# Twenty one-hot comparisons of each index search, moved from VectorE to GpSimd

## The chip, the cores and the metric
The kernel runs on one core of one Trainium2 chip. The metric is the device time of one execution in microseconds (us); lower is better. The kernel before took 3496.7 us (median of three runs, 3490.24 to 3497.87).

A core has five engines with a queue of instructions each: PE (TensorE, matrix products), DVE (VectorE), ACT (ScalarE), POOL (GpSimd) and SP (SyncE, which only starts transfers here). Each works its own queue in order; between engines only semaphores order the work.

## The reference
```python
scores = jnp.einsum('bhqd,bhkd->bhqk', q, k) * scale       # b=2, h=16, 4096 x 4096
sparsity = scores.max(axis=-1) - scores.mean(axis=-1)
_, top_idx = jax.lax.top_k(sparsity, U)                    # U = 307 queries of 4096
q_sel = jnp.take_along_axis(q, top_idx[..., None], axis=2)
scores_sel = jnp.einsum('bhud,bhkd->bhuk', q_sel, k) * scale
attn = jax.nn.softmax(scores_sel, axis=-1)
out_sel = jnp.einsum('bhuk,bhkd->bhud', attn, v)
out = jnp.zeros_like(q).at[bi, hi, top_idx].set(out_sel)
...
x = _layernorm(x + attention)
x = _layernorm(x + feed_forward(x))                        # token shift, sigmoid gate, squared relu
```
For each of the 32 pairs of batch and head the full score matrix is needed only for its row maxima. The 307 best queries are then found, attended for and written back.

## The kernel before
**Rounds.** The score matrices are worked through in 2048 rounds ("main" in the plan), 64 for a head. One round is a tile of 128 queries by 2048 key columns, folded into half of that: PE makes two products into CP (line 592) and two into DP (line 596), ACT takes the absolute value of CP into AB (line 858, two of 128x512), and DVE forms the sum of DP and AB and its maximum along the row in one instruction (line 1014, called the reduction here, 128x1024). AB has three buffers and DP two, so the engines can be only a few rounds apart. One reduction in each round makes the start of line 1014 a clock for the whole kernel.

**Beside the rounds** the function `schedule` writes out one plan, a list of tokens; every engine walks through it and emits what it has to do for each token. Between two rounds stand at most a few tokens from three generators: `selection` (the search for the 307 queries), `attention`, and `background` (projections, values, and the feed-forward part of batch 0). The heads are split into seven groups of 8, 5, 3, 5, 5, 3 and 3. A group's search starts when its last row maximum is there. Groups 0 to 5 are searched beside the rounds; group 6 is searched behind the last of them, in the tail.

**The search** (`select`) finds the cut value digit by digit (ACT compares, PE counts), marks the chosen queries, and ranks them by prefix sums on PE. The rank minus one is the slot of a query, 0 to 306. `slots` splits it: slot & 15 into fb, slot >> 4 into fa, both 128 partitions by 32 x n columns, where n is the group's number of heads: 256, 160, 96, 160, 160 and 96 columns for groups 0 to 5. Then come the one-hot tables: `ob` writes 16 comparisons of fb with 0 to 15 into OB on DVE (line 1144), which POOL multiplies by the token number (line 1360); `oa` writes 20 comparisons of fa with 0 to 19 into OA (line 1149). Beside the rounds both come two to a round: eight rounds of `ob`, then ten of `oa`. Four rounds later `idx` multiplies OA by OB on PE (line 667, 32 small products for a head), which puts each token number in its slot; the first of them waits for all of `sel_tk` and `sel_oa`. DVE adds an offset (line 1155), and `ixdma` stores the indices. SCR is the memory in which OA, OB and the attention buffers EL lie.

**Attention** for a head takes one step of 128 keys in a round: PE makes scores (line 688), ACT takes exponentials (line 896), POOL subtracts the upper half of each number to keep the rest as a second f16/bf16 operand (line 1411, EL), and six steps later PE multiplies both with the values (lines 703, 704). There are ten buffers. At the end of a head DVE normalizes (1170 to 1176), POOL adds a bias (1420) and starts three indirect DMAs (1424). `qgzero`, once, clears two areas of SCR on POOL (1368, 1369) behind group 0's search.

**Feed-forward beside the rounds** (`feed`, batch 0): a tile of 128 tokens advances by one stage in some nine rounds. POOL has most of its elementwise work: token shift (1475, 1477, 1480), squared relu (1490), normalization (1430 to 1435, 1462, 1511), sums (1445, 1498). PE's projection (726, W_rT) waits for the token shift (`f_mx`), and POOL's 1490 waits for ACT's relu (942). These stages run beside the searches of groups 3 and 4; attention runs beside those of groups 1, 2 and 5.

POOL's queue is ordered by the plan too. Within a round the tokens of `selection` stand ahead of those of `attention` or `background`. In group 3 the token shift of tile 13 stands ahead of the first comparison, and that of tile 14 behind the 18th. In group 4 the token shift of tile 28 stands ahead of all, and that of tile 29 behind the 14th.

Of the kernel before, what the change touches and what calls it, by code (L numbers as in the profile page):

```python
# [9 lines left out]
ALU = mybir.AluOpType  # L10
ACT = mybir.ActivationFunctionType

NB, L, D, H, DH = 2, 4096, 256, 16, 16
NT = L // 128
# [7 lines left out]
GROUPS = [(0, 0, 8), (0, 8, 5), (0, 13, 3), (1, 0, 5), (1, 5, 5), (1, 10, 3), (1, 13, 3)]  # L22
# [32 lines left out]
def schedule():  # L55
# [9 lines left out]
    def bank():  # L65
        while True:
            state["turn"] += 1
            b = spare[state["turn"] % len(spare)]
            if b != state["open"]:
                return b  # L70
# [49 lines left out]
    def select(g):  # L120
        n = GROUPS[g][2]
        gaps = 0 if tail[0] else 1
        on = "D" if tail[0] else "A"
        yield [("flip", g, bank())]
        for _ in range(gaps):
            yield []
        yield [("parts", g)]
        for _ in range(2 * gaps):
            yield []
        for i, (_, w) in enumerate(DIGITS):  # L130
            if gaps:
                for j in range(w):
                    yield [("cmp", g, i, j, on)] + ([("sel", g, i)] if j == 0 and i < n else [])
            else:
                yield [("cmp", g, i, j, on) for j in range(w)] + ([("sel", g, i)] if i < n else [])
            bk = bank()
            yield [("cnt", g, i, bk), ("digit", g, i, on, bk)]
            for _ in range(gaps):
                yield []
        for _ in range(2 * gaps):  # L140
            yield []
        yield [("cut", g, bank())]
        for _ in range(3 * gaps):
            yield []
        yield [("need", g, bank())]
        yield [("rank1", g, bank())]
        for _ in range(4 * gaps):
            yield []
        yield [("rank2", g, bank())]
        yield [("slots", g)]  # L150
        for _ in range(3 * gaps):
            yield []
        m = 2 if gaps else 4
        for j in range(0, 16, m):
            yield [("ob", g, j, m)]
        for j in range(0, A_COLS, m):
            yield [("oa", g, j, m)]
        for _ in range(4 * gaps):
            yield []
        for h in range(n):  # L160
            yield [("idx", g, h, bank())]
        yield [("ixdma", g)]
# [96 lines left out]
    def selection():  # L259
        for g in range(len(GROUPS)):  # L260
            while ("c", g) not in done or "p1" not in done:
                yield None
            state["search"] = True
            yield from select(g)
            state["search"] = False
            yield from prelude(g)
# [7 lines left out]
    for n in range(NB * H):  # L274
# [21 lines left out]
        if n + 1 in HEAD0:  # L296
            g = HEAD0.index(n + 1) - 1
# [20 lines left out]
def attention_rwkv(nc, x, Wq, bq, Wk, bk, Wv, bv, Wo, bo, W_r, W_k, W_v, mu_r, mu_k, out):  # L318
    ctx = ExitStack()
    with ctx:  # L320
        def sb(name, shape, dt=F32):
            return ctx.enter_context(nc.sbuf_tensor(name, shape, dt))

        def sem(name):
            return ctx.enter_context(nc.semaphore(name))
# [43 lines left out]
        OA = SCR[:, 2048:4608].bitcast(F16).rearrange("p (a n) -> p a n", a=A_COLS)  # L369
# [3 lines left out]
        fa = sb("fa", [128, NT * 8], F16)  # L373
        fb = sb("fb", [128, NT * 8], F16)
        SPr = sb("SPr", [128, NT, 8, 2])
        SB = [sb(f"S{g}", [128, 2, n, 16]) for g, (_, _, n) in enumerate(GROUPS)]
        SS = [v[:].rearrange("p u h t -> p u t h") for v in SB]
        slotf = sb("slotf", [128, NT, 8])
# [35 lines left out]
        def ff_tiles(count, w=D):  # L414
# [40 lines left out]
        sel_sl, sel_f, sel_ob, sel_tk, sel_oa, sel_ix = (sem(n) for n in (  # L455
            "sel_sl", "sel_f", "sel_ob", "sel_tk", "sel_oa", "sel_ix"))
        arr, ah_pe, ah_act, s_pe, ex_act, el_g, el_d = (sem(n) for n in (
            "arr", "ah_pe", "ah_act", "s_pe", "ex_act", "el_g", "el_d"))
# [496 lines left out]
        def _(dve):  # L955
# [138 lines left out]
            def cut(g, bank):  # L1094
                n, _, (m1, m2, *_) = views(g)
                cf = BANK[bank][:, 0:16 * n].rearrange("p (h q) -> p h q", q=16)[:, :, 0]
                cf = cf.unsqueeze(1).unsqueeze(1).broadcast_to([128, 2, 16, n])
                m1, m2 = (m.rearrange("p (u t) h -> p u t h", u=2) for m in (m1, m2))
                dve.wait_ge(sel_pe, SEL0[g] + 18)
                after(dve, sel_m, 5 * g)  # L1100
                dve.tensor_tensor(m1, SS[g], cf, ALU.is_gt).then_inc(sel_m, 1)
                dve.tensor_tensor(m2, SS[g], cf, ALU.is_equal).then_inc(sel_m, 1)
# [6 lines left out]
            def rank1(g, bank):  # L1109
                n, _, (m1, m2, m3, *_) = views(g)  # L1110
                dve.wait_ge(sel_m, 5 * g + 3)
                dve.wait_ge(sel_pe, SEL0[g] + 20)
                q = seq.mark(dve.tensor_tensor(m3, BANK[bank][:, 0:NT * n].rearrange("p (t h) -> p t h", h=n),
                                               need[:, 0:n].unsqueeze(1).broadcast_to([128, NT, n]), ALU.is_le))
                dve.wait_ge(q_dve, q)
                q = seq.mark(dve.tensor_tensor(m3, m3, m2, ALU.mult))
                dve.wait_ge(q_dve, q)
                dve.tensor_tensor(m3, m3, m1, ALU.add).then_inc(sel_m, 1)
# [24 lines left out]
                for j in range(j0, j0 + m):  # L1143
                    dve.tensor_scalar(OB[:, j, 0:NT * n], fb[:, 0:NT * n], float(j), None, ALU.is_equal).then_inc(sel_ob, 1)

            def oa(g, j0, m):
                n = GROUPS[g][2]
                for j in range(j0, j0 + m):
                    dve.tensor_scalar(OA[:, j, 0:NT * n], fa[:, 0:NT * n], float(j), None, ALU.is_equal).then_inc(sel_oa, 1)

# [95 lines left out]
            def f9(b, t, late):  # L1246
                if late:
# [5 lines left out]

            stages = dict(xt=xt, kbar=kbar, kmm=kmm, split=split, val=val, main=main, cap=capture, parts=parts, cmp=cmp,
                          digit=digit, cut=cut, need=need_, rank1=rank1, rank2=rank2, slots=slots, ob=ob, oa=oa, idx=idx,
                          st=st, otr=otr, f2=f2, f3=f3, f5=f5, f7=f7, f8=f8, f9=f9)
            for stage, *args in plan:
# [4 lines left out]
        def _(pool):  # L1262
# [91 lines left out]
            def ob(g, j0, m):  # L1354
                n = GROUPS[g][2]
                tk = tokc[:].unsqueeze(2).broadcast_to([128, NT, n])
                for j in range(j0, j0 + m):
                    v = OB[:, j, 0:NT * n].rearrange("p (t h) -> p t h", h=n)
                    pool.wait_ge(sel_ob, 16 * g + j + 1)
                    pool.tensor_tensor(v, v, tk, ALU.mult).then_inc(sel_tk, 1)  # L1360

            def qgzero():
                pool.wait_ge(l_s[0], 32 * 24)
                pool.wait_ge(l_s[1], 32 * 24)
                pool.wait_ge(l_q, 16 * 16)
                pool.wait_ge(xt_pe, 32)
                pool.wait_ge(s_lo, 48)
                pool.memset(QG, 0.0)
                pool.wait_ge(q_pool, seq.mark(pool.memset(QST, 0.0)))
# [136 lines left out]
            def f9(b, t, late):  # L1506
                if not late:
# [2 lines left out]
                    pool.wait_ge(f_r2, k + 1)  # L1510
                    pool.tensor_scalar(fo[k % 4], fo[k % 4], r[:, 0:1], r[:, 1:2], ALU.mult, ALU.add).then_inc(f_o3, 1)

            stages = dict(vones=vones, qzero=qzero, split=split, slots=slots, ob=ob, qgzero=qgzero, gath=gath, arr=arrange,
                          st=st, put=put, f1=f1, f2=f2, f3=f3, f5=f5, f6k=f6k, f7=f7, f8=f8, f9=f9)
            setup()
            for stage, *args in plan:
# [153 lines left out]
```

## Time and profile before
| | us |
|---|---|
| median of three runs (range) | 3496.7 (3490.24 to 3497.87) |
| profiled execution | 3497.08 |
| its span, first to last instruction | 3495.3 |
| PE busy | 3113.3 (89%) |
| DVE busy | 2940.5 (84%) |
| ACT busy | 2878.4 (82%) |
| POOL busy | 1491.0 (43%) |
| mean granted clock of PE, share of full speed | 0.968 |

Busy time counts the time in which an engine runs an instruction. A share over the whole span hides that each stretch has its own bound, and a wait inside an instruction, such as one for a shared port, counts as busy. Times in a timeline are counted from the start of the span.

### The profile page before, as it was taken

Reading aid. Unit: us, or ns where it says so; the run is one execution under the profiler, and the core shown is the slowest. Engines: PE = TensorE matmul, PEld = TensorE weight load, DVE = VectorE, ACT = ScalarE, POOL = GpSimd, SP = SyncE. Lnnn points to the kernel's source line nnn. Section 1 sums busy time; section 2 is a strip of 40 time slices with the busy share of each in tenths; the row PEclk is TensorE's granted clock in tenths of the full one; section 3 lists DMA queues with packets and bytes.
Section 4 is the critical chain, followed back from the end, with each engine's and each line's share of the span. In section 5 each row is a group of like instructions: output and inputs, shape, how many; then the busy total and the mean of one; then the engine's idle time right before and its main releaser. Section 6 shows DMA issues by size and latency. Waiting matters only on the chain.

```text
span 3495.3 us, 58965 instructions
## 1 busy us (share of the span) xinstructions
PE 3113.3 (89%) x15985; PEld 1442.4 (41%) x15985; DVE 2940.5 (84%) x5954; ACT 2878.4 (82%) x6445; POOL 1491.0 (43%) x2634
## 2 busy tenths in 40 slices
PE   5999999998899998998999888899988898897588
PEld 3334333343244433433444444544444443344366
DVE  2889988899978888888898888888887888886478
ACT  3889888889779999899899877699976699894455
POOL 2210022100136643453556455675555653457754
PEclk8999999999989999999999999999999999997899
DMA  6432232316122241241111241121141222013022
GB/s 183 147 81 36 61 85 76 82 36 15 25 38 38 38 33 27 37 33 31 23 38 29 43 48 42 42 44 36 31 38 42 40 32 31 14 20 15 14 77 69
DMA packets 262295, 163.64 MB, mean 47 GB/s; under 512 B 167563, under 2 KB 241483, under 8 KB 257867
## 3 DMA queue, kind: packets, MB, share of 16 engines
q1 hardware_dynamic: 255819, 158.50, 24.8%
q0 software_dynamic: 6144, 1.37, 0.5%
q8 instruction: 128, 2.10, 0.3%
q14 instruction: 204, 1.67, 0.2%
HBM read 111.86 MB, written 47.86 MB: 46 GB/s over the span
## 4 chain that ended last, share of the span: by engine, by line
PE 32%; ACT 26%; issue 19%; DVE 19%; POOL 2%; DMA 1%; SPq 0%; DVEq 0%; ACTq 0%; POOLq 0%
ACT AB L858 19%; DVE JK L1014 11%; PE CP L592 10%; PE DP L596 9%; ACT E L896 4%; ACT msk L879 2%; PE PV L703 2%; PE PV L704 2%; PE BP L688 2%; DVE SPr L1014 1%; PE PV L540 1%; DVE fst L1184 1%; PE BP L726 1%; PE BP L540 1%; DVE VF L1222 1%
## 5 line engine op out<-in xcount | busy, mean ns | idle before, releaser
L1014 DVE CUSTOM_DVE_ANT_0 JK<-DP,AB 128x1024 bf16<-128x1024 f32 x2048 | 2469.0, 1222 | 384.7 <-DVE SPr L1014 137.7
L858 ACT ACTIVATE AB<-CP 128x512 f32<-128x512 f32 x4096 | 2227.3, 598 | 306.8 <-PE CP L592 253.6
L592 PE MATMUL CP<-KS,QS 128*128 128x512 f16 x4096 | 1425.3, 389 | 96.3 <-ACT AB L858 20.5
L596 PE MATMUL DP<-KS,QS 128*128 128x512 f16 x4096 | 1241.9, 385 | 70.4 <-DVE SPr L1014 63.7
L1411 POOL TENSOR_TENSOR SCR<-E 128x307 f16<-128x307 f32 x968 | 672.5, 706 | 590.7 <-ACT E L896 581.8
L592 PEld LDWEIGHTS CP<-KS,QS 128*128 128x128 f16 x4096 | 393.8, 97 | 883.7 <-ACT AB L858 762.3
L596 PEld LDWEIGHTS DP<-KS,QS 128*128 128x128 f16 x4096 | 361.6, 98 | 402.9 <-DVE SPr L1014 187.3
L896 ACT ACTIVATE E<-BP 128x307 f32<-128x307 f32 x883 | 384.5, 436 | 55.1 <-PE BP L688 53.7
L1266 POOL TENSOR_SCALAR SCR<-SCR 128x48 f16<-128x48 f16 (+2 forms) x122 | 49.6, 406 | 571.7 <-DVE SCR L982 321.6
L688 PE MATMUL BP<-QT,KA 128*128 128x307 f16 x883 | 263.1, 298 | 20.9 <-ACT QT L888 19.1
L703 PE MATMUL PV<-E,XT 128*128 128x307 bf16 x512 | 161.4, 316 | 34.2 <-POOL SCR L1411 34.0
L1014 DVE DVE_READ_ACCUMULATOR2_ANT SPr<- 128x1 f32 x2048 | 168.9, 82 | 0.0
L704 PE MATMUL PV<-SCR,XT 128*128 128x307 f16 x512 | 157.6, 308 | 0.0
L703 PE MATMUL PV<-E,VF 128*128 128x307 bf16 x512 | 153.9, 301 | 0.0
L704 PE MATMUL PV<-SCR,VF 128*128 128x307 f16 x512 | 149.7, 292 | 0.0
L688 PEld LDWEIGHTS BP<-QT,KA 128*128 128x128 f16 x883 | 87.0, 98 | 147.3 <-issue 24.2
L1384 POOL DMA_INDIRECT SCR<-QN,idxs x96 | 99.6, 1037 | 77.2 <-issue 70.4
L1424 POOL DMA_INDIRECT AO<-OG,idxs x96 | 100.8, 1050 | 34.1 <-issue 16.9
L896 ACT ACTIVATE E<-DP 128x307 f32<-128x307 f32 x115 | 47.4, 427 | 48.3 <-PE DP L688 48.1
L1430 POOL TENSOR_SCALAR frs<-fmv 128x1 f32<-128x1 f32 x128 | 29.1, 227 | 132.3 <-DVE fmv L1186 129.6
L703 PEld LDWEIGHTS PV<-E,XT 128*128 128x128 f16 x512 | 52.1, 102 | 80.4 <-POOL SCR L1411 32.7
L1431 POOL TENSOR_TENSOR frs<-frs,halfc 128x1 f32<-128x1 f32 x128 | 78.3, 612 | 10.7
(381 smaller groups left out, 2984.5 us busy)
## 6 DMA issues: line engine op xcount, KB each, us to landing
KS<-KTC SPq DMA_DIRECT2D x256, 128.0 KB, 5.0
QS<-QSC SPq DMA_DIRECT2D x512, 64.0 KB
KA<-KTC SPq DMA_DIRECT2D x128, 128.0 KB, 3.8
QN<-SCR SPq DMA_DIRECT2D x16, 544.0 KB, 3.4
SCR<-in_L_attn_x SPq DMA_DIRECT2D x16, 512.0 KB, 6.8
KTC<-SCR SPq DMA_DIRECT2D x32, 256.0 KB, 2.2
QSC<-SCR SPq DMA_DIRECT2D x32, 256.0 KB, 2.3
AO<-E SPq DMA_DIRECT2D x2, 4096.0 KB, 21.9
```

The source lines that it names most:

```text
L592: pe.matmul(o, qs, ks[j][:, 1, :], start=True, stop=True).then_inc(sc_c, 1)
L596: r = pe.matmul(o[:, 512 * j:512 * j + 512], qs, ks[j][:, 0, :], start=True, stop=True)
L688: pe.matmul(o[:, 0:U], KA[hx % 2][:, 128 * kc:128 * kc + 128], QT[hx % 2][:, 0:U], start=True, stop=True).then_inc(s_pe, 1)
L703: pe.matmul(PV[:, 0:U], v, EH[a % NE], start=kc == 0, stop=False)
L704: pe.matmul(PV[:, 0:U], v, EL[a % NE], start=False, stop=kc == NT - 1).then_inc(pv_pe, 1)
L858: act.activation(AB[p % 3][:, 512 * j:512 * j + 512], BANK["C%d" % j], ACT.Abs).then_inc(ab_full, 1)
L896: act.activation(E[a % NE][:], BANK[bank][:, 0:U], ACT.Exp, scale=2 * SCALE / (WS * WS)).then_inc(ex_act, 1)
L1014: dve.tensor_tensor_reduce(out=JK[p % 2][:], in0=BANK["D%d" % u], in1=AB[p % 3][:], scale=1.0, scalar=-3.0e38, op0=ALU.add, op1=ALU.max, a ...
L1384: pool.indirect_dma_start(out=QG[0:w, 3 * (hx % 8) + c, :], out_offset=None, in_=QNr[b], in_offset=bass.IndirectOffsetOnAxis(ap=ixf[0:w, k ...
L1411: pool.tensor_tensor(EL[a % NE], E[a % NE][:], EH[a % NE], ALU.subtract).then_inc(el_g, 1)
L1424: pool.indirect_dma_start(out=AOr[b], out_offset=bass.IndirectOffsetOnAxis(ap=ixf[0:w, k:k + 1], axis=0), in_=OG[i][0:w, c, :], in_offset= ...
L1431: i = pool.tensor_tensor(r[:, 0:1], r[:, 0:1], halfc[:], ALU.pow)
```

## The change
The 20 comparisons of `oa` go from DVE to POOL in groups 0 to 5. The plan stays as it is but for a flag in the token: "A" beside the rounds, "D" in the tail. DVE skips the token where the flag is "A"; POOL skips it where it is "D". On POOL each `oa` token first waits for fa and fb, which POOL itself writes. The 16 comparisons of `ob` stay on DVE.

```diff
         for j in range(0, A_COLS, m):
-            yield [("oa", g, j, m)]
+            yield [("oa", g, j, m, on)]
...
-            def oa(g, j0, m):
+            def oa(g, j0, m, on):
                 n = GROUPS[g][2]
+                if on == "A":
+                    return
                 for j in range(j0, j0 + m):
                     dve.tensor_scalar(OA[:, j, 0:NT * n], fa[:, 0:NT * n], float(j), None, ALU.is_equal).then_inc(sel_oa, 1)
...
+            def oa(g, j0, m, on):
+                n = GROUPS[g][2]
+                if on == "D":
+                    return
+                pool.wait_ge(sel_f, g + 1)
+                for j in range(j0, j0 + m):
+                    pool.tensor_scalar(OA[:, j, 0:NT * n], fa[:, 0:NT * n], float(j), None, ALU.is_equal).then_inc(sel_oa, 1)
```
POOL's table of stages gets the new function as well.

## Rows read from the trace of the kernel before

**Rows 1.** The page, its first part: busy us (share of the span) xinstructions.
```profile
PE 3113.3 (89%) x15985; PEld 1442.4 (41%) x15985; DVE 2940.5 (84%) x5954; ACT 2878.4 (82%) x6445; POOL 1491.0 (43%) x2634
```

**Rows 2.** Windows of groups 0 to 5: length, busy PE PEld DVE ACT POOL, clock, DMA.
```profile
939.40:956.50 17.10, 11.97 (x41) 3.48 (x40) 17.08 (x42) 10.85 (x21) 4.17 (x4) 0.90 0.00 1
1418.60:1436.40 17.80, 13.87 (x65) 5.17 (x63) 17.73 (x46) 14.39 (x30) 10.33 (x15) 1.00 0.02 3
1710.60:1725.30 14.70, 14.06 (x68) 6.07 (x69) 14.59 (x44) 13.83 (x31) 7.59 (x11) 1.00 0.01 2
2221.20:2238.50 17.30, 14.34 (x67) 7.24 (x66) 17.20 (x48) 12.00 (x26) 14.29 (x35) 1.00 0.07 23
2730.40:2748.90 18.50, 15.47 (x63) 7.62 (x62) 17.25 (x47) 11.57 (x25) 15.66 (x37) 0.91 0.04 15
3034.50:3051.60 17.10, 14.53 (x63) 6.55 (x64) 15.17 (x42) 11.54 (x25) 9.73 (x21) 0.80 0.00 1
```

**Rows 3.** The same view: four plain rounds of group 0; ten rounds with attention.
```profile
956.50:961.07 4.57, 3.99 (x25) 1.38 (x24) 4.57 (x8) 3.72 (x7) 0.00 (x0) 1.00 0.00 0
1746.37:1759.85 13.48, 13.44 (x72) 6.23 (x72) 12.32 (x21) 13.40 (x31) 11.32 (x27) 1.00 0.54 80
```

**Rows 4.** Timeline of group 0: start, us, engine, line, operation (idle before in brackets).
```profile
940.55 3.19 DVE L1149 TENSOR_SCALAR SCR<-fa 128x256 f16<-128x256 f16 x2
...
940.94 2.66 POOL L1369 MEMSET SCR<- 128x3072 f16 x1
...
953.67 1.22 DVE L1014 CUSTOM_DVE_ANT_0 JK<-DP,AB 128x1024 bf16<-128x1024 f32 x1
...
955.08 1.22 DVE L1014 CUSTOM_DVE_ANT_0 JK<-DP,AB 128x1024 bf16<-128x1024 f32 x1
```

**Rows 5.** Timeline of group 1: DVE beside POOL.
```profile
1419.53 2.67 POOL L1411 TENSOR_TENSOR SCR<-E 128x307 f16<-128x307 f32 x4
...
1420.86 1.21 DVE L1014 CUSTOM_DVE_ANT_0 JK<-DP,AB 128x1024 bf16<-128x1024 f32 x1
...
1431.96 1.08 POOL L1424 DMA_INDIRECT AO<-OG,idxs  x1 [0.30 <-issue]
...
1432.31 2.82 DVE L1149 TENSOR_SCALAR SCR<-fa 128x160 f16<-128x160 f16 x2
```

**Rows 6.** Timeline of group 5: its first pair of comparisons.
```profile
3035.69 1.62 DVE L1149 TENSOR_SCALAR SCR<-fa 128x96 f16<-128x96 f16 x2
```

**Rows 7.** Groups by form on POOL: count | busy us, mean ns | idle before.
```profile
L1431 POOL TENSOR_TENSOR frs<-frs,halfc 128x1 f32<-128x1 f32 x128 | 78.3, 612 | 10.7
L1360 POOL TENSOR_TENSOR SCR<-SCR,tokc 128x160 f16<-128x160 f16 x48 | 20.9, 459 | 3.8 <-DVE SCR L1144 2.4
L1332 POOL TENSOR_SCALAR SCR<-SCR 128x512 f16<-128x512 f16 x12 | 7.4, 618 | 0.0
L1266 POOL TENSOR_SCALAR fa<-sloti 128x160 f16<-128x160 int32 x3 | 1.0, 325 | 14.8 <-DVE sloti L1133 14.8
```

**Rows 8.** Timeline of group 1: a subtraction, its first use, the first index matmul.
```profile
1412.85 0.70 POOL L1411 TENSOR_TENSOR SCR<-E 128x307 f16<-128x307 f32 x1
...
1418.84 0.30 PE L703 MATMUL PV<-E,VF 128*128 128x307 bf16 x1
...
1442.45 1.54 PE L667 MATMUL BP<-SCR 128*20 128x16 f16 x32
```

**Rows 9.** Timeline of groups 3 and 4: POOL's token shift and the matmul behind it.
```profile
2234.06 0.61 POOL L1490 TENSOR_TENSOR VF<-VF 128x256 f32<-128x256 f32 x1 [1.95 <-ACT VF L942]
...
2238.48 0.73 POOL L1480 TENSOR_TENSOR VF<-VF 128x256 f32<-128x256 f32 x1
...
2242.20 0.41 PEld L726 LDWEIGHTS BP<-W_rT,VF 128*128 128x128 f32 x2
...
2740.47 0.61 POOL L1490 TENSOR_TENSOR VF<-VF 128x256 f32<-128x256 f32 x1 [1.48 <-ACT VF L942]
...
2745.73 0.67 PE L726 MATMUL BP<-W_rT,VF 128*128 128x256 f32 x2 [0.43 <-POOL VF L1480]
```

## What the change does to the time, predicted

> **What bounds the kernel now.** I read the page first: in 3495.3 us TensorE (PE) is busy 89%, VectorE (DVE) 84%, ScalarE (ACT) 82% and GpSimd (POOL) 43% [rows 1]. An average like this names no bound, so the stretches in which the 120 moved comparisons stand come next. There is one for each of the groups 0 to 5, ten rounds long, with two comparisons in each round; the view of windows gives the busy time of each engine in them [rows 2]. DVE is busy 17.08 of 17.10 us in group 0, 17.73 of 17.80 in group 1, 14.59 of 14.70 in group 2, 17.20 of 17.30 in group 3. There it is DVE that ends last. In groups 4 and 5 it has gaps (17.25 of 18.50, 15.17 of 17.10). POOL is the other column to read: 4.17, 10.33 and 7.59 us in groups 0 to 2, 9.73 in group 5, but 14.29 and 15.66 us in groups 3 and 4, because the feed-forward part of batch 0 runs on it at that time.
>
> Then I asked what a round costs once the comparisons are gone. Right behind the comparisons of group 0, four rounds take 4.57 us, 1.14 each: the reduction alone, back to back [rows 3]. With attention beside it ten rounds take 13.48 us, and ACT is busy 13.40 of them, so 1.35 a round is ACT's pace [rows 3]. Those are the two floors.
>
> **What the change removes.** Undisturbed, a round with two comparisons of 256 columns takes 1.41 us from one reduction to the next (953.67 to 955.08), and one without takes 1.14 [rows 3, 4]. The disturbed ones are worth more. In group 0 one pair is 3.19 us long, while POOL clears two areas, the larger in 2.66 us [rows 4]. In group 1 one pair takes 2.82 us while POOL works through four subtractions without a gap [rows 5]. In group 5 the first pair takes 1.62 us [rows 6].
> A page of the Trainium skill (SBUF — State Buffer, "SBUF: two separate sides") says that a DVE operation which uses both ports and a POOL instruction exclude each other for one whole instruction. The trace agrees that they exclude each other, but the pair in group 1 waits for about three of POOL's instructions, not one. By the page it would have cost about 1.3 us less, and the gain there would be smaller by as much. The measured pair is the one I use.
> POOL's comparisons should not hold up the reductions that stay on DVE: the one at 1420.86 starts while POOL is inside four subtractions in a row and takes its usual 1.21 us [rows 5].
>
> Group by group, from the length of the stretch now to the length after:
> - Group 0, no attention beside it: 17.1 us become ten rounds of 1.14, 11.4. **Minus 5.6.** POOL does its 20 comparisons first (8 us at the price below, to about 949) and clears afterwards, when DVE has no comparison left to block. The index matmuls come four rounds behind the stretch, 939.4 + 11.4 + 4.6 = 955.4, well behind POOL's last comparison.
> - Group 1: 17.8 become 13.5 at ACT's pace [rows 2, 3]. **Minus 4.3.**
> - Group 2: 14.7 become 13.5. **Minus 1.2.**
> - Group 5: the pair of 1.62 us goes, less 0.1 that it overlaps with its neighbours and the 0.2 by which ACT's floor lies above DVE's (1.35 against 1.14): **minus 1.3**. A plain pair of 96 columns fits between the two floors, so the other nine rounds gain nothing; much of this stretch is at a low clock (0.80 on the mean [rows 2]) and PE's.
>
> **What it adds.** POOL has no comparison with a constant in this trace, and no operation of one step on more than two columns. Its one-input operations of two steps cost 325 ns at 160 columns and 618 at 512 [rows 7], 0.83 ns a column. I take 0.34 us at 160, 0.28 at 96 and 0.40 at 256, the line through these two rows and a little for the other form. Below, I see 0.29. Above stands the two-input product of 160 columns at 459 ns [rows 7]; and the power function, at 612 ns for a single column [rows 7], shows that the kind of operation can matter on POOL, so a tail reaches to 0.7. All in all POOL gets 60 x 0.34 + 40 x 0.28 + 20 x 0.40, near 40 us. What matters is where POOL is late.
> The Trainium skill (GPSIMD Engine Reference, Elementwise) gives about 1.8 cycles for an element at best, and 769 ns for 512 elements. This case's 128x512 row says 618 [rows 7], faster. By the page 160 columns would be near 0.42 us (an estimate) and the sum below near minus 5.2 us.
>
> - Groups 1, 2, 5: a step of attention asks POOL for one subtraction (four in 2.67 us, 0.67 each [rows 5]); with two comparisons that is 1.35 in a round of 1.35. POOL neither falls behind nor catches up. The subtraction that ended at 1413.55 is first used by the matmul at 1418.84 [rows 8], so 5 us of delay cost nothing. The index matmuls of group 1, which now wait for POOL's comparisons, start at 1442.45 [rows 8]. POOL works from 1419.5 through 20 comparisons (6.8), some nine subtractions (5.9) and an addition with three indirect DMAs of 1.08 and gaps of 0.3 (4.5 [rows 5]) and is done near 1436.7, while PE comes there near 1438.2 (1442.45 - 4.3). **Nothing added**, but with 1.5 us to spare only.
> - Group 3: PE waits for POOL at the projection of each feed-forward tile (line 726 behind line 1480). Two such hand-overs lie around the stretch. The earlier one has none of the new comparisons in front of it in POOL's queue. In front of the later one stand 18. Now it ends on POOL at 2239.21 (2238.48 + 0.73) and is used at 2242.20, 3.0 us of slack, and POOL waited 1.95 us for ACT on the way there [rows 9]. 18 x 0.34 = 6.1, less 1.95 of idle time, puts the end at 2243.4: PE is 1.3 us later than before, though DVE was relieved of 20 comparisons. **Plus 1.3.**
> - Group 4: the same hand-over has no slack at all. PE waits already now for POOL (0.43 us, released at 2745.7), and POOL idled 1.48 us on the way [rows 9]. 14 comparisons precede it: 14 x 0.34 = 4.8, less 1.48. **Plus 3.3.** The index matmuls of groups 3 and 4 stand behind these hand-overs in PE's queue and come later by the same amount, which leaves POOL the time for its last two to six comparisons.
> The later hand-overs come behind the index matmuls, which hold up PE and let POOL catch up, so the delay isn't paid twice. The tail (group 6) keeps its comparisons on DVE.
>
> **Sum.** -5.6 - 4.3 - 1.2 - 1.3 + 1.3 + 3.3 = -7.8 us. The profiled execution took 3497.1 us (a span of 3495.3 and 1.8 around it), against a median of 3496.7 for the three timed runs: 3497.1 - 7.8 = **3489.3 us**. A difference under 0.2%, 7 us, can hardly be told from no change here, and the forecast lies just beyond that.
>
> **Rivals.**
> 1. *POOL is never late.* If the feed-forward hand-overs absorb the delay, because POOL's work in front of them shrinks or PE is held up elsewhere, groups 3 and 4 gain too: 17.3 and 18.5 us become about 14.6 and 15.5, which is PE's busy time there (14.34 and 15.47 [rows 2]). That gives -12.4 - 2.7 - 3.0 = -18.1, 3479.0 us. Against it speak the 0.43 us wait and POOL's 15.66 us of work in 18.50. Chance 0.13.
> 2. *The comparison is dearer, slower than before.* Groups 3 and 4 pay 18 + 14 = 32 comparisons of 160 columns: each 0.1 us more costs 3.2 us. From 0.42 the margin in group 1 is gone too: PE then waits in front of the index matmuls for POOL's last comparison, and 20 x (price - 0.42) of the gain there goes, up to all 4.3. At 0.459 the sum is -7.8 + 3.8 + 0.8 = -3.2 us (3493.9); at 0.52 it is zero, and from there on the kernel is slower. At 0.7 it is -7.8 + 11.5 + 4.3 = +8.0, 3505 us. One mechanism: POOL's queue sets when PE goes on. For it speaks that no such operation is in the trace and the row of 612 ns; against it, that all wide one-input rows lie on one line. Chance of a price of 0.42 to 0.52: 0.18; above it 0.11, of which 0.08 lie over 0.67, where the loss reaches 7 us.
> 3. *The change does nothing.* If every round were held by ACT or PE at the same time and DVE's busy time only looks full, the time stays 3497. The 3.19 and 2.82 us pairs, in which PE stood still, speak against it. Chance 0.06.
> The forecast has 0.52, and carries its own spread of some 4 us: the granted clock falls to half in many short stretches (0.90 to 0.91 on the mean in groups 0 and 4, 0.80 in group 5 [rows 2]), and new waits of PE in groups 3 and 4 may add such a fall, the one avoided in group 0 take one away.
>
> **Range and chances.** From rival 1 to just short of the dearest comparison: 3478 to 3500 us. Faster by over 0.2% (under 3489.7): 0.13 of rival 1 and 0.38 of the forecast's 0.52 (more than half, for its spread reaches further down, to falls of the clock that are avoided), 0.51. Slower by over 0.2% (above 3503.7): 0.08. The same: 0.41, from the rest of the forecast, the price of 0.42 to 0.67 and rival 3.
>
> **What would show each step.** In the profile after, rounds of 1.14 us in group 0's stretch and no DVE instruction over 2 us there; ten rounds near 13.5 us in groups 1 and 2; POOL's comparisons of 160 columns at 0.34 us; waits of PE line 726 for POOL line 1480 grown from 0.43 us to 3 or more in group 4 and new in group 3, and ten rounds of groups 3 and 4 longer than before. The prediction is wrong if POOL's comparison costs 0.45 us or more, if PE's index matmuls wait for it, or if the feed-forward hand-overs show no wait.

## The result, and the profile after

The changed kernel takes 3520.4 us (median of four runs, 3519.8 to 3523.5) against 3495.9 for the kernel before beside it: a ratio of 1.0074, 95% interval 1.0057 to 1.0092. It is slower by 24.5 us in the medians, 26 by the ratio, where 7.8 us less were forecast. The profiled execution has a span of 3518.0 us against 3495.3.

The page after, busy time of the engines, answers to [rows 1]:

```profile
PE 3120.8 (89%) x15985; PEld 1444.1 (41%) x15985; DVE 2920.8 (83%) x5834; ACT 2876.4 (82%) x6445; POOL 1561.6 (44%) x2754
```

120 instructions went from DVE to POOL. DVE is busy 20 us less and POOL 71 us more, where the prediction had added 40. The groups by form on POOL (count | busy us, mean ns | idle before) say why. Line 1370 is the moved comparison, 1362 the product that was line 1360:

```profile
L1370 POOL TENSOR_SCALAR SCR<-fa 128x160 f16<-128x160 f16 x60 | 36.5, 612 | 3.9
L1362 POOL TENSOR_TENSOR SCR<-SCR,tokc 128x160 f16<-128x160 f16 x48 | 20.9, 459 | 3.8 <-DVE SCR L1144 2.4
L1370 POOL TENSOR_SCALAR SCR<-fa 128x96 f16<-128x96 f16 x40 | 18.0, 452 | 2.6
L1370 POOL TENSOR_SCALAR SCR<-fa 128x256 f16<-128x256 f16 x20 | 16.9, 847 | 1.3
```

A comparison of 160 columns costs 612 ns, not 340; from 96 to 256 columns it grows by 2.5 ns a column, where the line through [rows 7] grows by 0.83. That line also left out rows of the kernel before (count | busy us, mean ns | idle before):

```profile
L1475 POOL TENSOR_SCALAR VF<-VF,cols 128x128 f32<-128x128 f32 x128 | 47.8, 374 | 0.0
L1462 POOL TENSOR_SCALAR VF<-VF,frs 128x256 f32<-128x256 f32 x32 | 17.6, 552 | 0.1
```

Both are multiply-adds too, but with a factor read from a column of memory instead of a constant. By the line they would cost 298 and 404 ns. So it was not true that all wide one-input rows lie on one line, which rival 2 had as its reason against a dearer comparison.

Next the windows of the same ten rounds in groups 0 to 5, which answer to [rows 2] (length; busy PE, PEld, DVE, ACT, POOL with counts; clock, DMA share, GB/s):

```profile
938.80:950.20 11.40, 10.18 (x40) 2.93 (x38) 11.40 (x20) 10.27 (x20) 10.77 (x14) 1.00 0.00 0
1418.20:1431.50 13.30, 12.89 (x63) 5.44 (x62) 12.55 (x26) 12.51 (x28) 12.09 (x21) 1.00 0.01 2
1714.90:1728.50 13.60, 13.30 (x65) 5.68 (x66) 12.74 (x25) 12.87 (x29) 11.88 (x24) 1.00 0.00 1
2227.20:2241.80 14.60, 13.70 (x65) 7.10 (x64) 13.73 (x28) 11.59 (x25) 13.39 (x30) 1.00 0.06 20
2743.60:2768.90 25.30, 15.54 (x60) 7.39 (x59) 13.94 (x28) 10.68 (x23) 23.12 (x48) 0.80 0.02 6
3056.80:3072.40 15.60, 14.30 (x63) 6.53 (x64) 12.29 (x22) 11.36 (x25) 13.98 (x33) 0.79 0.00 2
```

The relief of DVE came as forecast: 17.1 us became 11.4 in group 0 (11.4 forecast), 17.8 became 13.3 in group 1 (13.5), 14.7 became 13.6 in group 2 (13.5). Group 3 even became shorter here, 14.6 instead of 17.3. Only group 4 pays in its own stretch, 25.3 instead of 18.5. The other losses stand behind the stretches. To see them, take the start of the same reduction in both traces; the shift after minus before is -0.6 us when the ranks of group 0 are ready, and then:

| from the start of the group's slots to the next group's | forecast | changed kernel |
|---|---|---|
| group 0 | -5.6 | +0.2 |
| group 1 | -4.3 | +4.7 |
| group 2 | -1.2 | +1.7 |
| group 3 | +1.3 | +7.3 |
| group 4 | +3.3 | +9.0 |
| group 5 and the tail | -1.3 | +0.4 |
| sum | -7.8 | +23.3 |

One trace isn't exact to the microsecond here: in two later runs whose groups 0 to 2 are those of the kernel before, the same three lines read -1.0, +3.2, +2.4 and +2.3, +0.3, +0.9. The timed runs by groups, below, are the firmer evidence.

The waits of the changed kernel (engine, line, waited for: us in total, times, longest) name the places:

```profile
PE PV L703 <- POOL SCR L1421: 37.4, 7, 11.0
PE PV L726 <- POOL VF L1500: 14.0, 2, 7.1
PE BP L667 <- POOL SCR L1370: 6.8, 3, 3.8
PE BP L726 <- POOL VF L1490: 3.3, 5, 1.1
```

and those of the kernel before:

```profile
PE PV L703 <- POOL SCR L1411: 34.0, 6, 10.9
PE BP L726 <- POOL VF L1480: 2.4, 3, 1.2
PE BP L726 <- POOL VF L1490: 1.7, 1, 1.7
```

New are 14 us in which PE waits for line 1500, the squared relu (1490 before), once in group 3 and once in group 4, 6.8 us in which the index matmuls wait for the comparisons, and 3.4 us for attention's subtractions. The token shift (1490, was 1480), on which the prediction set its two losses, grew by 0.9 us only.

The timeline of group 3 after (start, us, engine, line, operation, idle time before in brackets):

```profile
2243.35 5.40 POOL L1370 TENSOR_SCALAR SCR<-fa 128x160 f16<-128x160 f16 x8
...
2248.83 0.61 POOL L1500 TENSOR_TENSOR VF<-VF 128x256 f32<-128x256 f32 x1
...
2249.59 1.19 PE L726 MATMUL PV<-W_vT,VF 128*128 128x256 f32 x2 [6.94 <-POOL VF L1500]
...
2255.49 0.67 PE L726 MATMUL BP<-W_rT,VF 128*128 128x256 f32 x2 [0.70 <-POOL VF L1490]
...
2257.55 1.51 PE L667 MATMUL PV<-SCR 128*20 128x16 f16 x32 [0.54 <-POOL SCR L1370]
```

Eight comparisons in a row, 5.40 us, are 0.68 apart, more than their 0.61. Behind them stands the square for which PE has been waiting 6.9 us. By the time of the projection on which [rows 9] rest (2242.20 before, 2255.46 after) the rounds have lost what the forecast allowed for and 6 us more.

In groups 0 and 1 it is the index matmuls and a subtraction:

```profile
949.82 8.25 POOL L1370 TENSOR_SCALAR SCR<-fa 128x256 f16<-128x256 f16 x9
...
958.22 1.42 PE L667 MATMUL BP<-SCR 128*20 128x16 f16 x32 [3.83 <-POOL SCR L1370]
...
1438.54 0.42 PE L703 MATMUL PV<-E,VF 128*128 128x307 bf16 x1 [3.51 <-POOL SCR L1421]
...
1442.18 1.51 PE L667 MATMUL BP<-SCR 128*20 128x16 f16 x32 [1.27 <-POOL SCR L1370]
```

### The profile page after: what moved, and what is told of

Read it like the earlier page. It is cut to its first block, busy times and chain, and to the rows that moved or that the text cites. A ratio compares the mean times of both kernels' runs of the same rounds, so it can differ in the third digit from the quotient of the medians.

```text
span 3518.0 us, 58965 instructions
## 1 busy us (share of the span) xinstructions
PE 3120.8 (89%) x15985; PEld 1444.1 (41%) x15985; DVE 2920.8 (83%) x5834; ACT 2876.4 (82%) x6445; POOL 1561.6 (44%) x2754
## 4 chain that ended last, share of the span: by engine, by line
PE 25%; ACT 17%; issue 15%; DVE 11%; POOL 4%; DMA 1%; DVEq 0%; ACTq 0%; POOLq 0%; SPq 0%
ACT AB L858 11%; PE CP L592 8%; PE DP L596 7%; DVE JK L1014 5%; ACT E L896 3%; PE PV L703 2%; PE PV L704 2%; PE BP L688 2%; ACT msk L879 1%; POOL SCR L1370 1%; DVE fst L1186 1%; PE BP L726 1%; DVE VF L1224 1%; PE PV L726 1%; DMA SCR<-QN,idxs 1%
## 5 line engine op out<-in xcount | busy, mean ns | idle before, releaser
L688 PEld LDWEIGHTS BP<-QT,KA 128*128 128x128 f16 x883 | 86.9, 98 | 146.3 <-issue 25.5
```

Source lines behind the costliest of these rows:

```text
L688: pe.matmul(o[:, 0:U], KA[hx % 2][:, 128 * kc:128 * kc + 128], QT[hx % 2][:, 0:U], start=True, stop=True).then_inc(s_pe, 1)
```

## The experiments

Ratios are against the kernel before on the same chip, with their 95% interval; shifts are those of the reductions in the traces.

**What makes POOL's comparison dear.** Nothing of the network is left; ten one-input forms and a two-input product, six each at four widths (the loop is shortened here).

```diff
+for form in (one_cmp, one_mul, cmp_add, mul_add, sub_max, mul_cmp, cmp_mul, one_ge, one_max, cmp32, tt_mul):
+    for w in (96, 160, 256, 512):
+        for k in range(6): form(w)      # e.g. pool.tensor_scalar(out, in, 3.0, None, ALU.is_equal)
```

> Nothing of the network is computed here: x is copied to the output while POOL runs rows of one-input operations of ten forms and one two-input product, six of each at 96, 160, 256 and 512 columns. It asks what makes POOL's comparison dear (612 ns at 160 columns in the changed kernel, where 325 was the row for a multiply-add). Theory A, the one-step form is dear: a product with one constant costs what the comparison costs, near 0.61 us at 160, and a comparison followed by adding zero falls to 0.33. Theory B, comparing is dear: a one-step product costs 0.33 or less, and a comparison costs 0.6 with or without a second step. Theory C, both go through one slow routine and only multiply-add is quick: every form but multiply-add costs 0.6.

The groups by form at 160 columns (and two at 512). Line 47 is the comparison as the change writes it, 50 a product with one constant, 53 comparison then add, 56 multiply-add, 74 a maximum in one step, 77 the two-input product:

```profile
L47 POOL TENSOR_SCALAR BB<-A 128x512 f16<-128x512 f16 x6 | 8.7, 1486 | 0.1
...
L53 POOL TENSOR_SCALAR BB<-A 128x160 f16<-128x160 f16 x6 | 4.3, 747 | 0.1
...
L56 POOL TENSOR_SCALAR BB<-A 128x512 f16<-128x512 f16 x6 | 3.5, 617 | 0.1
L50 POOL TENSOR_SCALAR BB<-A 128x160 f16<-128x160 f16 x6 | 3.5, 607 | 0.1
...
L47 POOL TENSOR_SCALAR BB<-A 128x160 f16<-128x160 f16 x6 | 3.5, 606 | 0.1
...
L74 POOL TENSOR_SCALAR BB<-A 128x160 f16<-128x160 f16 x6 | 3.5, 604 | 0.1
...
L77 POOL TENSOR_TENSOR BB<-A,C 128x160 f16<-128x160 f16 x6 | 2.7, 485 | 0.1
...
L56 POOL TENSOR_SCALAR BB<-A 128x160 f16<-128x160 f16 x6 | 1.8, 325 | 0.1
```

Theory C holds. The price has nothing to do with comparing: a product with one constant costs the same 0.61 us. Multiply followed by add is the one quick form among the ten; every other form of one step costs 2.5 ns a column, and every other of two steps more, 747 ns at 160. All wide one-input rows of the kernel before were multiply-adds, and the line was drawn through those of them that have two constants: a special case. The run doesn't try multiply-adds with a column as factor.

**The comparison in two steps.**

```diff
-pool.tensor_scalar(OA[:, j, 0:NT * n], fa[:, 0:NT * n], float(j), None, ALU.is_equal)
+pool.tensor_scalar(OA[:, j, 0:NT * n], fa[:, 0:NT * n], float(j), 0.0, ALU.is_equal, ALU.add)
```

> The changed kernel with POOL's comparison written in two steps, is_equal and then add 0.0; the values are the same. Theory A (the one-step form is dear): 0.33 us at 160 columns, and by the sum of the prediction near -8 us against the kernel before, 3489. Theories B and C: the price stays near 0.61 us or rises, and the time stays near 3520, or a little above.

755 ns at 160 columns, and 3539.3 us: 1.0125 (1.0108 to 1.0142). 0.14 us more on each of 60 comparisons, 0.22 on 20 and 0.09 on 40 are 16.6 us of POOL, and the kernel loses another 16 to 19. So where POOL is late already, more of its time goes into the kernel's nearly in full.

**The price that was forecast.**

```diff
-pool.tensor_scalar(OA[:, j, 0:NT * n], fa[:, 0:NT * n], float(j), None, ALU.is_equal)
+pool.tensor_scalar(OA[:, j, 0:NT * n], fa[:, 0:NT * n], 0.0, 0.0, ALU.mult, ALU.add)
```

> The changed kernel with each of POOL's 120 comparisons replaced by a multiply-add with 0.0 of the same shape (the price that the prediction took, 0.33 us at 160 columns). The upper part of the slots then isn't computed, and in groups 0 to 5 the 307 first tokens are attended for instead of the chosen ones, with the same number of transfers. If the prediction failed in the price alone, this takes 3497 - 8 = 3489 us, with group 3 about 1 and group 4 about 3 us later than before. If taking work off DVE costs something by itself (an order of waits, falls of PE's clock), it stays above 3497.

0.9962 (0.9949 to 0.9976), 13.3 us less than before. POOL's operations cost 329, 276 and 413 ns. (In groups 0 to 5 the table is then all zeros, and the indices are the constants that the iota behind it gives.) This is the prediction with its price right: the forecast of 3489.3 was 5.6 us too high for it, 3483.7. From here to the changed kernel POOL's 120 operations cost 35.5 us more, and the kernel takes 37 to 39 more, again nearly one for one. Group by group the shifts are -4.3, -3.8, -0.1, -1.9, +3.8 and, in group 5 with the tail, -5.4. Group 4 loses as forecast (+3.3); group 3 gains where a loss of 1.3 was forecast, and group 5 gains 4 us more, but 3.3 of its gain come before its comparisons begin, so not from the change.

**DVE relieved, POOL nearly free.**

```diff
+if (g, j0) == (0, 0):
+    pool.wait_ge(q_pool, seq.mark(pool.memset(OA[:], 0.0)))
-pool.tensor_scalar(OA[:, j, 0:NT * n], fa[:, 0:NT * n], float(j), None, ALU.is_equal)
+pool.memset(OA[:, j, 0:1], 0.0)
```

> As the run with multiply-adds, but each of POOL's 120 operations is the clearing of a single column (about 0.1 us), and the table is cleared once, in group 0. This is what the relief of DVE is worth when POOL pays almost nothing. The prediction's first rival gives -18 us, 3479; if ACT or PE hold the rounds at the same time, less than 5 us are gained.

0.9956 (0.9939 to 0.9972), 3483.6, 14 to 15 us less than before: as much as with multiply-adds, so in the total POOL's part at 0.33 us was hidden. The interval reaches from 10 to 21 us and doesn't exclude the first rival's 18. The trace, with 11.1 us less, is below it: the ten rounds are 14.6 us long in group 3, as that rival had it, and 16.1 in group 4, where it had 15.5. In group 4 POOL's part does show: -1.1 us here against +3.8 with multiply-adds. These two runs also change the data (a table of zeros, the iota as in the run before); what that does by itself wasn't tested, but the mean granted clock is 0.968 in both, as before.

**Which groups lose.**

```diff
-yield [("oa", g, j, m, on)]
+yield [("oa", g, j, m, "D" if g in (3, 4) else on)]        # POOL in 0, 1, 2, 5
+yield [("oa", g, j, m, "D" if g in (0, 1, 2, 5) else on)]  # POOL in 3 and 4
```

> POOL makes the comparisons in groups 0, 1, 2 and 5, beside which only attention runs; in groups 3 and 4, beside the feed-forward stages, they stay on DVE. If the loss of each group is its own, this keeps 0.8 + 4.8 + 1.6 + 0.3 = +7.5 us of the changed kernel's 22.7 (shift of the rounds, from the two traces): 3504 us. If the loss sits in the feed-forward hand-overs alone, as the prediction had it, the time is 3490 or less.

> The complement: POOL makes the comparisons in groups 3 and 4 alone. If losses add up: +7.3 and +7.5 and some 1 us behind group 4, near +15 us, 3512. The price of 0.61 us in the prediction's own sum gives 18 x 0.61 - 1.95 - 3.0 = +6.0 for group 3 and 14 x 0.61 - 1.48 = +7.1 for group 4, +13 us together, 3510. If the loss were one of clock or of order that any shift of the plan brings, it would be far from both.

The first: 1.0026 (1.0016 to 1.0035), +9 us. The second: 1.0048 (1.0031 to 1.0065), +17 us; its trace loses 5.0 us in group 3 and 9.0 in group 4, against 7.3 and 9.0 in the changed kernel. The two add up to 1.0074, the whole change. So two thirds of the loss belong to groups 3 and 4, with the feed-forward hand-overs, and one third to groups that the prediction had as gains of 12.4 us.

**Clearing later.**

```diff
 def qgzero():
     ...
+    pool.wait_ge(sel_oa, A_COLS)
     pool.memset(QG, 0.0)
```

> The kernel before, with one wait more on POOL: it clears its two areas only when DVE's 20 comparisons of group 0 are through. Tests what the 3.19 us pair is worth: if it is a wait for POOL's clearing and on the path, the pair shrinks to 0.35 us and the time falls by 2.8 us, to 3494. If PE's stall there was covered by something later (the falls of the clock, the index matmuls), less than 1 us is gained.

0.9995 (0.9985 to 1.0004): no difference that this can tell, though the interval reaches to 5 us less and doesn't exclude the 2.8 expected. In the trace the long pair is 0.35 us like its neighbours and the stretch 2.9 us shorter, so the pair did wait for POOL's clearing. What follows it is larger than the effect: the eight rounds with the index matmuls of group 0, windows before, after and here:

```profile
961.07:984.03 22.96, 22.96 (x282) 13.78 (x281) 10.81 (x27) 8.70 (x16) 0.00 (x0) 0.67 0.32 59
```

```profile
954.79:984.17 29.38, 25.95 (x289) 14.62 (x290) 11.14 (x26) 8.68 (x16) 6.08 (x6) 0.54 0.24 45
```

```profile
958.50:976.70 18.20, 18.20 (x281) 12.89 (x278) 10.44 (x26) 7.91 (x15) 0.00 (x0) 1.00 0.16 45
```

The last column but two is the granted clock, 0.67, 0.54 and 1.00 of full speed (2.4 GHz; it falls to 1.2). The same eight rounds take 22.96 us, 29.38 with 3.83 of waiting in them, and 19.14 (to the end of the eighth; the window shown ends 0.9 us earlier). At full clock they would be 3.8 us shorter in the kernel before, and 6.4 in the changed one, after its wait is taken out. The run with POOL in groups 3 and 4 alone, whose group 0 is that of before, took 19.2 us as well; the one with half the comparisons of groups 3 and 4 on POOL, unchanged here too, took 24.7 at a clock of 0.56. So this stretch's time varies from run to run with the clock, by 5.5 us, without any change to it. All 14 traces of the network together: in the 11 in which no index matmul of group 0 waits for POOL, the eight rounds take 19.1 to 24.7 us at clocks of 1.00 to 0.56; in the three with such a wait (the changed kernel, the one in two steps, and POOL in groups 0, 1, 2 and 5) they take 25.5 us beside the wait, at 0.53 to 0.55. In the five index rounds of group 1 the 11 have 12.2 to 15.2 us at 1.00 to 0.60, the three 17.8 to 18.3 at 0.50.

**One comparison each, in groups 0, 1, 2 and 5.**

```diff
-for j in range(j0, j0 + m):      # DVE
+for j in range(j0, j0 + m, 2 if on == "A" else 1):
-for j in range(j0, j0 + m):      # POOL
+for j in range(j0 + 1, j0 + m, 2):
```

Groups 3 and 4 have the flag "D" (all on DVE), DVE's early return is gone, and POOL clears behind the comparisons as in the run before.

> In groups 0, 1, 2 and 5 each round gives one comparison to DVE and one to POOL, groups 3 and 4 stay on DVE, and POOL clears behind the comparisons. By rates alone both engines now fit in a round: POOL 0.67 + 0.59 = 1.26 us, DVE 1.14 + 0.15 = 1.29, ACT 1.35. Then group 0 gains 4.5 (rounds of 1.28, and no 3.19 us pair), group 1 some 4, groups 2 and 5 one to three each: -9 to -12 us, 3486. If DVE's remaining comparisons now wait for POOL's slow ones (they exclude each other, 0.6 us each), nothing is gained: 3495 or more.

0.9969 (0.9959 to 0.9979), 10.8 us less. The first expectation was right: the ten rounds are 14.1 us long in group 1 and 13.9 in group 2, a little over ACT's pace, so DVE's remaining comparisons do wait at times, but cheaply.

**The index matmuls later.**

```diff
-for _ in range(4 * gaps):
+for _ in range(12 * gaps):       # between oa and idx, in the changed kernel
     yield []
```

> The changed kernel with twelve empty rounds instead of four between a group's comparisons and its index matmuls. If PE's waits for POOL in front of the index matmuls (3.8 us in group 0, 1.3 in group 1) and the falls of its clock behind them are a cause, groups 0 and 1 give back some 6 and 4 us, and groups 3 and 4, whose loss sits at feed-forward hand-overs, stay at about +7 each: 3520 - 8 = 3512 us. If the index matmuls were slow for another reason, the rows behind them stay as long as in the changed kernel and the time at 3520. Starting attention eight rounds later in each group may cost some of it in the tail.

1.0009 (0.9999 to 1.0020), 3498.6: better than either theory said. No index matmul waits for a comparison any more, and by the start of group 3 the rounds are 19 us ahead of before where the changed kernel is 6 behind. 11 us of that are given back behind the last reduction; that attention, started later, is left over is the likely reason. Groups 3 and 4 lose 3.7 and 8.6 us, nearly as before in group 4. The kernel is 22 us faster than the changed one without those waits, so they and what follows them are the likely cause in groups 0 to 2; part of the 19 us is only work put off, and this run doesn't separate them.

**One comparison a round on POOL in groups 0, 1, 2 and 5.**

```diff
-for j in range(0, A_COLS, m):
-    yield [("oa", g, j, m, on)]
+slow = on == "A" and g not in (3, 4)
+for j in range(0, A_COLS, 1 if slow else m):
+    yield [("oa", g, j, 1 if slow else m, "A" if slow else "D")]
```

> In groups 0, 1, 2 and 5 POOL makes one comparison a round over twenty rounds instead of two over ten; groups 3 and 4 stay on DVE. POOL then needs 0.67 + 0.61 = 1.28 us a round with attention, less than ACT's 1.35, where two comparisons need 1.9. If POOL's rate against the round is what decides, the subtractions stay in time, the waits in front of the index matmuls go, and the gain predicted for these groups appears: -5.6 - 4.3 - 1.2 - 1.3 = -12.4, near 3487. If one comparison a round is still too much, or the search that is ten rounds longer holds up attention, 3495 or more.

0.9965 (0.9951 to 0.9979), 3484.0. POOL's comparison is as dear as ever (618 ns at 160 columns), but fits in a round. The control, with the same spread on DVE, and a repetition beside it:

```diff
-for j in range(0, A_COLS, m):
-    yield [("oa", g, j, m)]
+slow = on == "A" and g not in (3, 4)
+for j in range(0, A_COLS, 1 if slow else m):
+    yield [("oa", g, j, 1 if slow else m)]
```

> The kernel before with DVE making one comparison a round over twenty rounds in groups 0, 1, 2 and 5; POOL makes none. It is the control for the run in which POOL makes one a round (ratio 0.9965): is it the spreading that gains, or the engine? By rates, a round beside attention becomes 1.14 + 0.15 = 1.29 us of DVE, under ACT's 1.35, so groups 1 and 2 gain their undisturbed part as well; group 0, where nothing else bounds, keeps its 20 comparisons on the path, and pairs that meet POOL's instructions still wait. If the engine matters: -2 to -5 us, 3493 to 3496. If spreading is all: -12 us, as there.

> The run in which POOL makes one comparison a round in groups 0, 1, 2 and 5, once more beside the control: 0.9965 again, 3485 us, if the first result holds. If it was chance, nearer to 1.

The control: 0.9986 (0.9976 to 0.9997), 3 to 5 us less. The repetition: 0.9959 (0.9943 to 0.9976), 3482.8 us, 14 less than before. So about a third of the gain comes from spreading, two thirds from the engine. This is the fastest version that computes the whole reference, ahead of both kernels.

Where the gain arises is less clear than the sum. In the traces nearly all of it stands in group 0: -16.9 and -13.1 us in the two with POOL, -6.1 in the control. Groups 1 and 2 show -0.5 and -1.7, -1.1 and -1.7, and in the control -1.1 and +1.1, so the 4.3 us forecast for group 1 did not appear. Part of group 0's figure is attention put off, since the search ends ten rounds later: behind the last reduction 7.3, 5.3 and 8.1 us are given back. Part is the clock, at 1.00, 0.67 and 0.56 in its index rounds.

**One each in groups 3 and 4 only.** The edit is that of the one-each run, with the flag turned round and POOL's clearing where it was.

> In groups 3 and 4 each round gives one comparison to DVE and one to POOL; all other groups stay on DVE. With both on POOL these groups cost +18.9 us. If the loss is what is left over when POOL's added time exceeds the slack at the hand-overs of squared relu and token shift (3.9 and 3.0 us with 1.95 us of idle time in group 3, 0.7 and 0.1 with 1.48 in group 4), halving the comparisons does much better than halving the loss: group 3 adds 8 x 0.65 - 1.95 - 3.9 < 0, group 4 7 x 0.65 - 1.48 = +3: +1 to +3 us in all, about 3500. If each comparison on POOL costs its time, as when the engines simply exclude each other, half the loss remains, +9, 3508.

1.0018 (1.0008 to 1.0028), 6 us more. In the trace group 3 loses 3.0 us and group 4 2.5, together 5.5 where the full move loses 14 to 16: little more than a third for half of the comparisons. That is between the two theories: less than half the loss, so slack absorbs some of it, but more than the +1 to +3 expected. (The 18.9 us of the expectation is the whole shift in the trace with POOL in groups 3 and 4; 4.6 of it stand in groups 0 to 2, which that run doesn't change.)

## Why the prediction was wrong

- *What bounds the kernel, and the relief of DVE:* right. DVE ended last in groups 0 to 3 (with POOL nearly free the ten rounds fall to 11.4, 13.3, 13.6 and 14.6 us), the lengths of the stretches came out within 0.2 us of the forecast in groups 0, 1 and 2, no reduction was held up by POOL (the longest takes 1.23 us, as before), and with the forecast price the kernel is 13 us faster. Its sizes were off for groups 3 and 5, the sum by 5 to 6 us, on the careful side.
- *The price of POOL's comparison:* the step that failed. "[...] the line through these two rows and a little for the other form" gave 0.34 us; it measured 0.612. Both rows were multiply-adds with constants, and the run of forms shows that this is the only quick one of ten. Two other rows of the same trace, 374 ns at 128 columns and 552 at 256, lay above the line. The rival had it as a tail with a chance of 0.11 for more than 0.52. The prediction even noted that no one-step operation on more than two columns was in the trace; that was a reason to put the weight on the bound of 0.459 and above.
- *What the dearer price costs:* too small by a factor. At 0.612 the prediction's own formula is -7.8 + 32 x 0.27 + 20 x 0.19 = +4.7 us; +23 came. For groups 3 and 4 the formula gives 18 x 0.612 - 1.95 - 3.0 = +6.1 and 14 x 0.612 - 1.48 = +7.1, 13.2 against 16.3. It is near, though PE stopped at another hand-over: the squared relu (line 1490 before), which stands behind 16 comparisons in group 3 and 12 in group 4. Its former end, 2234.67, had 3.9 us of slack; the prediction looked at the token shift alone. The comparisons are also up to 0.68 us apart rather than 0.59.
- *Groups 0, 1, 2 and 5:* the larger miss, -8.6 by the same formula against +7.0. The mechanism of rival 2 was the right one (PE waits in front of the index matmuls for POOL: 3.8 us in group 0, 1.3 in group 1), and in group 1 the subtractions fell behind too, by more than their 5 us of slack, 3.5 us of waiting. But the rival counted the waits alone. In group 1 the rounds lose 9.3 us between the end of the comparisons and the last index matmul: 4.8 are the two waits, and 3.8 lie in the five index rounds, which without the wait in them take 16.5 us at a granted clock of 0.50, against 12.7 at 0.91 before. In group 0's eight rounds it is 25.5 us at 0.54 against 23.0 at 0.67. The clock was that low in all three traces with such waits and in none of the 11 without, but these 11 differ among themselves by 5.5 us in group 0 and 3 in group 1. So a low clock goes with the waits; that the waits bring it on is a conclusion, and how many microseconds of it are theirs stays open.
- *That nothing is paid twice:* half right. Group 3's loss is complete at its first index matmul (+6.7 of +7.3 there). Group 4's isn't: +6.6 there and +9.0 when group 5 starts; why the last 2.4 come isn't known.
- *A reading of [rows 5]:* the four subtractions shown at 1419.53 are not those beside the pair of 2.82 us. That pair starts at 1432.31, during an indirect DMA of POOL, and ends at 1435.13, behind the third of four subtractions that begin at 1433.06. The sum isn't touched by it.

What it would have taken: one look at which form the two rows share and at the rows off their line, and a forecast whose margins (1.5 us in group 1) hold at the bound of 0.459 and not only at the favoured value.

## What to carry to other kernels

A price taken from neighbouring rows holds for the same form only: on POOL a multiply-add costs 0.33 us where a product with one constant, or a comparison, costs 0.61. Work moved off the bound to an engine with 57% idle time costs nothing only if it fits where it stands: two comparisons a round lost 9 us in groups 0, 1, 2 and 5, one a round over twice the rounds gained 12 to 14, a third of that by the spreading alone. In front of a queue that a bound engine waits for, list every hand-over behind the new work, not the tightest one before the change, and look behind each new wait of PE at what its clock does next. Read the same stretch in several traces before a few microseconds of it are explained.

## What the runs showed of the hardware

- POOL's one-input instruction with constants has one quick form among the ten tried. At 512 columns multiply-add takes 617 ns and a comparison, product or maximum in one step 1483 to 1487; two steps of any other kind tried take 1917 to 1920. The comparison costs the same in f16 and f32. A two-input product (485 ns at 160 columns) is cheaper than a product with one constant (607). In the kernel before, multiply-adds with a column as factor cost 374 ns at 128 columns and 552 at 256.
- Successive slow instructions are up to 0.68 us apart in the kernel where each lasts 0.61, while in the run of forms they follow within 0.59.
- While POOL's instructions follow each other without a gap, a DVE comparison can wait through several of them: 2.15 us through three subtractions of 0.7 us at 1432.98 in the kernel before, and a pair of 3.19 us beside POOL's clearing is 0.35 us when POOL clears later.
- PE's clock in the eight index rounds of group 0 differs between executions in which nothing there was changed: 19.1 to 19.2 us at full clock, 22.96 where it is 0.67 on the mean, 24.7 where it is 0.56.
